# Longer lags in three attention stages of a four-layer transformer kernel

## The reference

```python
x = x + xattn0(norm(x), ctx, ctx, mask, bias)      # 16 heads, softmax, stage a0
x = x + rwkv_ffn(norm(x))                          # stage f0
x = x + gelu(norm(x) @ ctx.T) @ ctx                # stage m1
x = x + top2_experts(norm(x))                      # stages r1, e1
x = x + xattn2(norm(x), ctx, ctx, causal)          # 16 heads, stage a2
x = x + shared_ffn(norm(x)) + top1_expert(norm(x)) # stages r2, s2, e2
x = x + xattn3(norm(x), ctx, ctx)                  # scores that are 0 count as -1e30, stage a3
x = x + int8_linear(norm(x))                       # one scale for the whole tensor, stage q3

def xattn(x, ...):
    q, k, v = heads(x @ Wq), heads(ctx @ Wk), heads(ctx @ Wv)   # 16 heads of 16
    return softmax(q @ k.T / 4 + bias) @ v @ Wo
```

## Time and profile before

| | before |
|---|---|
| median of 3 runs | 1209.71 us (1206.89 to 1211.71) |
| the profiled execution | 1210.15 us, span 1208.4 us |
| mean granted TensorE clock | 0.853 of full speed |
| PE busy | 919.9 us, 76% |
| DVE busy | 578.3 us, 48% |
| ACT busy | 412.9 us, 34% |
| POOL busy | 403.8 us, 33% |

### The profile page before, as it was taken

The page is one execution under the profiler, slowest core; times in us unless marked ns, Lnnn a source line. Parts: engine busy times, 40 slices in busy tenths (PEclk is TensorE's granted clock), DMA queues, the critical chain, the costliest instruction groups (busy, mean ns, idle before and its releaser), DMA issues. The chain is left out here.

```text
span 1208.4 us, 18723 instructions
## 1 busy us (share of the span) xinstructions
PE 919.9 (76%) x5575; PEld 607.7 (50%) x5576; DVE 578.3 (48%) x1230; ACT 412.9 (34%) x804; POOL 403.8 (33%) x739
## 2 busy tenths in 40 slices
PE   7688758776249999945678749997999977787732
PEld 5465537642127777723455415564666664555511
DVE  4788835644322222227998532221111136768827
ACT  4345533322003233314666422221222216555610
POOL 5556635431560000036775211100000025555512
PEclk9799978968559999975988769998999968788955
DMA  5780000000121111127410030002111110000002
GB/s 166 263 295 2 1 22 26 0 9 0 66 91 52 63 63 61 61 68 261 175 32 10 1 107 30 22 18 66 44 46 50 40 28 15 14 15 6 1 1 69
DMA packets 60182, 71.25 MB, mean 59 GB/s; under 512 B 8171, under 2 KB 51923, under 8 KB 60115
## 3 DMA queue, kind: packets, MB, share of 16 engines
q1 hardware_dynamic: 55507, 57.81, 14.4%
q0 software_dynamic: 4608, 12.59, 3.2%
HBM read 45.73 MB, written 24.64 MB: 58 GB/s over the span
## 5 line engine op out<-in xcount | busy, mean ns | idle before, releaser
L1549 PE MATMUL PS<-WE,tmp 128*128 x496 | 185.8, 518 | 0.0
L1193 DVE TENSOR_TENSOR tmp<-PS,tmp 128x352 f32<-128x352 f32 (+1 forms) x78 | 47.4, 608 | 260.2 <-ACT tmp L851 260.2
L540 POOL TENSOR_TENSOR tmp<-tmp,small 128x616 f32<-128x616 f32 x96 | 116.5, 1214 | 107.3 <-DVE small L969 104.0
L505 POOL DMA_INDIRECT WE<-ys,slot_u x32 | 32.5, 1016 | 341.2 <-DMA ys<-tmp 335.3
L1549 PEld LDWEIGHTS PS<-WE,tmp 128*128 128x128 f32 x496 | 91.5, 194 | 60.4 <-issue 36.2
L764 ACT ACTIVATE tmp<-PS 128x768 f32<-128x768 f32 x96 | 77.8, 810 | 112.2 <-PE PS L1373 111.5
L851 ACT ACTIVATE tmp<-PS 128x352 f32<-128x352 f32 (+1 forms) x78 | 41.4, 530 | 218.7 <-PE PS L1549 218.7
L1569 PE MATMUL PS<-WE,tmp 128*128 (+1 forms) x418 | 101.0, 380 | 2.1 <-DVE tmp L1205 2.1
L1284 PE MATMUL PS<-ident,XN 128*128 128x128 f32 x240 | 49.5, 342 | 67.7 <-ACT XN L700 53.7
L1371 PE MATMUL PS<-ident,tmp 128*128 128x128 f32 x384 | 69.6, 311 | 40.1 <-POOL rsx L527 21.8
L635 POOL DMA_INDIRECT xs<-tmp,slot_u x48 | 46.5, 969 | 121.2 <-DVE tmp L1180 111.5
(11 more groups left out here) (204 smaller groups left out, 1623.6 us busy)
## 6 DMA issues: line engine op xcount, KB each, us to landing
tmp<-xs SPq DMA_DIRECT2D x62, 128.0 KB, 2.0
ys<-tmp SPq DMA_DIRECT2D x62, 128.0 KB, 1.7
xs<-WE SPq DMA_DIRECT2D x4, 1536.0 KB, 9.5
WE<-in_L_w SPq DMA_DIRECT2D x16, 352.0 KB, 7.1
WE<-in_L_rgT SPq DMA_DIRECT2D x8, 512.0 KB, 9.9
WE<-in_L_ruT SPq DMA_DIRECT2D x8, 512.0 KB, 10.0
WE<-in_L_rdT SPq DMA_DIRECT2D x8, 512.0 KB, 10.2
X<-in_x SPq DMA_DIRECT2D x8, 256.0 KB, 6.7
```

The source lines that it names most:

```text
L540: pool.tensor_tensor(sc, sc, spread(mx[:, q], SK), ALU.add).then_inc(shifted, 1)
L1193: dve.tensor_tensor(HH[:, q, 0:F], PS[:, 2 * q + 1, 0:F], SL[:, q, 0:F], ALU.mult).then_inc(hh_ready, 1)
L1549: last = pe.matmul(PS[:, 2 * q + k, 0:F], XS[:, q, c], w, start=c == 0, stop=c == G - 1)
```

## The change

The slot tables move. Transposes of a unit stand three slots after its scores instead of two, values five instead of three. The copy of the transposed values (ACT) goes to slot k+4. ACT empties `BANK_X` one slot after PE has filled it (`later(...)`), where it used to do so in the same slot; `out_projection` moves from 4b+7 to 4b+10 and so stands in the slot right behind `queries(b+3)`. Norms go one slot later than their statistics, and `XN` gets a second buffer. On POOL the shift of slot s goes ahead of the bias add and of the norm's arithmetic, and `MEANS` is written only for the output norms in `a2`. Gathers start one slot earlier, their add two slots earlier: in `a2` the last gather of batch entry b moves from slot 4b-8 to 4b-9, its add from 4b-6 to 4b-8. The value blocks of `a3` go from slot 0 to the slots -5 and -4 on PE and to -7 and -4 on DVE. No matmul or vector operation is added or taken away but 40 tiny copies to `MEANS`.

```diff
-        XN = sb("XN", [P, T, D])
+        XN = sb("XN", [P, 2, T, D])
...
         def queries_slot(b):
-            return UNITS * (b - 1) + 1
+            return UNITS * b - 3
         def out_proj_slot(b):
-            return UNITS * b + 7
+            return UNITS * b + 10
         def residual_slot(b):
-            return UNITS * b + 8
+            return UNITS * b + 11
         def deviations_slot(b):
-            return UNITS * b + 9
+            return UNITS * b + 12
+        def normalise_slot(b):
+            return UNITS * b + 13
         def transpose_slot(b):
-            return UNITS * b + 10
+            return UNITS * b + 15
         def gather_slot(b, t, k, K):
-            return UNITS * b - 11 + t * 2 + k * (2 // K)
+            return UNITS * b - 12 + t * 2 + k * (2 // K)
         def add_slot(b):
+            return UNITS * b - 8
+        def in_deviations_slot(b):
+            return UNITS * b - 7
+        def in_normalise_slot(b):
             return UNITS * b - 6
-        def in_deviations_slot(b):
-            return UNITS * b - 5
...
+        def later(slot_of):
+            return lambda b: slot_of(b) + 1
...
-                    bq = batch_at(queries_slot, s)
-                    if bq is not None and bq > 0 and stage != "a2":
-                        queries(bq)
...
-                    if 2 <= s < NU + 2:
-                        u = s - 2
+                    if 4 <= s < NU + 4:
+                        u = s - 4
                         act.wait_ge(pt_psum, u0 + u + 1)
                         after(act, ot_ready, (u0 + u) // 2 - 1 if u >= 4 else 0)
                         act.activation(PT[:, u % 4], PT_PSUM, ACT.Copy).then_inc(pt_ready, 1)
...
+                    bq = batch_at(later(queries_slot), s)
+                    if bq is not None and stage != "a2":
+                        queries(bq)
+                    for slot_of, which in ((later(in_transpose_slot), "in"), (later(transpose_slot), "out")):
...
-                    if s == 0 and stage == "a3":
-                        for i in range(B // 2):
-                            value_blocks(2, i)
+                    if stage == "a3" and s in (add_slot(0) + 1, add_slot(1)):
+                        for i in range(2):
+                            value_blocks(2, i if s < add_slot(1) else 2 + i)
...
-                    if 3 <= s < NU + 3:
-                        values(s - 3)
+                    if 5 <= s < NU + 5:
+                        values(s - 5)
...
-                    if 2 <= s < NU + 2:
-                        transposes(s - 2)
+                    if 3 <= s < NU + 3:
+                        transposes(s - 3)
```

More of the change, by code:

```diff
@@ L282, in slots_of @@
         def slots_of(stage):
-            return range(gather_slot(0, 0, 0, 1) if stage in FED_FROM else 0, transpose_slot(B - 1) + 1)
+            return range(gather_slot(0, 0, 0, 1) if stage in FED_FROM else queries_slot(0), later(transpose_slot)(B - 1) + 1)
         def norm_order(stage):
@@ L540, in attention @@
                         pool.tensor_tensor(sc, sc, spread(mx[:, q], SK), ALU.add).then_inc(shifted, 1)
+                    if j == 2 and 1 <= b <= B and stage != "a3":
+                        if stage in FED_FROM:
+                            pool.wait_ge(xn_ready, norms + order["in", b - 1] + 1)
+                        pool.tensor_tensor(x_of(b - 1), x_of(b - 1), repeat(rows[:, 1], T), ALU.add).then_inc(out_bias, 1)
+                    for slot_of, which in ((in_deviations_slot, "in"), (deviations_slot, "out")):
+                        bd = batch_at(slot_of, s)
+                        if bd is not None and (which, bd) in order:
+                            i = order[which, bd]
+                            deviations_and_shifts(norms + i, bd, shifts + i, stage == "a2" and which == "out")
                     if stage in FED_FROM:
@@ L764, in attention @@
                         act.activation(PT[:, u % 4], PT_PSUM, ACT.Copy).then_inc(pt_ready, 1)
[L765 to L768, removed]
-                        normalise(norms + i, bn, shifts + i, XN)
-                    bi = batch_at(in_deviations_slot, s)
-                    if bi is not None and stage in FED_FROM:
-                        i = order["in", bi]
-                        after(act, xt_psum, norms + i)
-                        if stage == "a3" and bi > 3:
-                            act.wait_ge(amax_taken, bi - 3)
-                        normalise(norms + i, bi, shifts + i, XN)
+                    bq = batch_at(later(queries_slot), s)
+                    if bq is not None and stage != "a2":
+                        queries(bq)
+                    for slot_of, which in ((later(in_transpose_slot), "in"), (later(transpose_slot), "out")):
+                        bt = batch_at(slot_of, s)
+                        if bt is not None and (which, bt) in order:
+                            xt_evacuate_at(norms + order[which, bt], bt)
+                    for slot_of, which in ((in_normalise_slot, "in"), (normalise_slot, "out")):
+                        bn = batch_at(slot_of, s)
+                        if bn is not None and (which, bn) in order:
+                            i = order[which, bn]
+                            after(act, xt_psum, norms + i - 1)
+                            if stage == "a3":
+                                after(act, amax_taken, sum(w == "out" for (w, _), n in order.items() if n <= i - 2))
+                            normalise(norms + i, bn, shifts + i, XN[:, i % 2])
                 end_stage(act, stage)
@@ L1403, in attention @@
                 for s in slots_of(stage):
-                    if s == 0 and stage == "a3":
-                        for i in range(B // 2):
+                    if stage == "a3" and s in (in_transpose_slot(0) - 1, in_transpose_slot(0)):
+                        for i in range(2) if s < in_transpose_slot(0) else range(2, 4):
                             pe.wait_ge(v_ready, B // 2 + i + 1)
                             value_blocks(2, i)
-                    if s == 0 and stage != "a2":
-                        queries(0)
                     if s == 0 and stage == "a3":
```

55 lines of the change are left out of this document (18 added, 37 removed).

## The result

| | before | after |
|---|---|---|
| median | 1208.36 us | 1259.97 us (1254.91 to 1267.59, 4 runs) |
| ratio after / before | | 1.0428, 95% interval 1.0362 to 1.0495 |
| the profiled execution | 1210.15 us | 1256.2 us, span 1254.5 us |
| mean granted TensorE clock | 0.853 | 0.830 |

What follows compares the result with a forecast made beforehand. It took `a0` as nearly TensorE's, `a2` as VectorE's and `a3` as a ring of waits. `a0` +6.8, `a2` +14.3, `a3` -13.4 and clock +12 gave +19.7 on 1210.15: 1229 us, range 1205 to 1244.

Steps and rivals of the forecast that it cites:

- The ring through the bank: Output projection waits for ScalarE to empty `BANK_X` behind exponential and copy: 15.6 us an entry in `a0`, 19.5 in `a3`.
- TensorE waits for the copy: Sign expected in the changed profile: TensorE's transposes wait for the ScalarE copy, 20 us and more in `a0`.
- the copy's own ring: Transposes wait for the copy behind the exponential, the next reciprocal sums for them: 3.16 us a slot, VectorE alone 2.56.
- The faster rival: Early copy removes TensorE's 0.43 us wait per unit if the exponential starts under about 1.4 us after B(s-1): 1188 us; 15%.
- The value blocks run at full clock: Start of `a3`: value blocks moved ahead of the rows take 6.9 us at full clock; first biased scores 11.2 us earlier.
- Unit 8 of `a2`: First stalls of `a2`, gathers under a weight load: unit 8 would come 6.7 us later.
- The step that failed in `a0`: Clock term of `a0`: taken as 0, with bounds of 0 and 4 us, as its gaps come apart.
- In `a3`, where the clock was booked at 9 us: Clock term of `a3`: a third of the time at half clock, 1.5 us by 6 entries, 9 us.
- Plain slots cost 0.5 and the projection 0.3 more: Entry of `a2`: these two costs beside the gather's stall; 16.65 us becomes 18.8.
- the stall is 1.4 us: Entry of `a2`: VectorE's add waits 1.4 us for the last gather, which has one slot to land instead of two.
- The ends: Ends of the three attentions: -1 us in `a0`, -1.5 in `a2`, -1 in `a3`.
- two without outputs: Entries of `a3` without outputs: 16.1 us each, where a full entry takes 19.5.

Runs made afterwards that it cites:

- filler: Changed kernel with four identity transposes added on TensorE beside the values in nearly every slot; 1234.56 us, 1.0213 of the kernel before.
- copy_mid: Changed kernel with ScalarE's copy, in `a2` alone, between the exponential and the two small copies; 1247.97 us, 1.0317 of the kernel before.
- both_undone: Changed kernel with `BANK_X` emptied in the slot of its fill, ahead of the copy, and the copy of unit s-3 in slot s; 1197.71 us.
- bank_same_slot: Changed kernel with ScalarE emptying `BANK_X` in the slot of its fill, still behind exponential and copy; 1219.02 us, 1.0101 of the kernel before.
- gap_filled: both_undone with 20 identity transposes in TensorE's long wait in five slots of `a2`; 1195.08 us, 0.986 of the kernel before.
- adds_one_later: both_undone with the adds of gathered rows, their statistics' rest and norm one slot later; 1182.39 us, 0.9772 of the kernel before.
- after_adds_later: Changed kernel with the adds of gathered rows, their statistics' rest and norm one slot later; 1254.17 us, 1.0367 of the kernel before.

## Why the forecast was wrong

**Right.** The ring through the bank, which runs through the copy in ScalarE's queue, is there with the size given: 15.8 us an entry in `a0` at full clock for 15.6, 19.15 and 19.36 in `a3` for 19.5. TensorE waits for the copy (19.5 us in `a0`, "20 us and more" was written). Whether the copy's own ring takes 3.16 us a slot no row shows by itself; at full clock it bound no full entry of `a0` (14.61 us with or without it). The faster rival failed by its own condition: the exponential starts 2.2 us after the end of the biased scores in the middle of `a0`, as before the change, where the rival needed 1.4. The value blocks run at full clock ahead of the rows, and bring 10.9 us for 11.2:

```profile
1017.68 1.03 PE L1328 MATMUL PS<-WE,firstrows 77*128 77x256 f32 x4
...
1024.92 1.03 PE L1328 MATMUL PS<-WE,leftrows 77*128 77x256 f32 x4
1025.78 0.60 PE L1285 MATMUL PS<-ident,XN 128*128 128x128 f32 x4
```

Unit 8 of `a2` is 6.3 us later for 6.7, in part by luck. By the forecast the fourth add would have begun 47.4 us behind the first gather, and unit 8 would have come 13.6 us behind it. The add began at 45.1 us, and the way from there to unit 8 took 15.5 us, at a clock of 0.50.

**The step that failed in `a0`: "In `a0` the clock was 1.00; bounds are 0 and 4 us (a third of 1.99 by 6), and I take 0, as its gaps come apart."** The clock of the kernel before was used for a kernel whose waits are longer. Four of the six windows from unit 8 on ran at 0.61 to 0.81. The term was 6.8 us by the run with filler, above even the upper bound, which had counted the projection alone: queries, transposes, scores and values double as well. In `a3`, where the clock was booked at 9 us, it measured 9.4.

The page TensorE: Matmul & The Clock Gate of the Trainium skill, on the second failure mode, had said what the rows of `a0` then showed: idle gaps between groups of matmuls make the clock swing. The forecast set it aside for the 1.00 of the earlier trace rows. Gaps alone don't decide, as the kernel before shows: with one of 0.43 us in every slot five entries in a row ran at 1.00.

**The step that failed in `a2`: "Plain slots cost 0.5 and the projection 0.3 more", and "the stall is 1.4 us".** Plain slots were priced by the ring of `a0`, with only the exponential ahead of the copy. ScalarE's small copies of `a2` stand ahead of it as well, and they wait for VectorE. That is 13.3 us by copy_mid, the fall of the clock behind this wait with it. The gather's stall, in exchange, is 0.2 us an entry behind unit 8 instead of 1.4: the longer entry gave the gather its time. Two errors of opposite sign left +6.1 where they met.

**The ends.** -1, -1.5 and -1 were credited for the tails; they came out at +0.7, +2.6 and +0.3. These three and the head of `a0` make some 7 us, and no row carried them. In `a3` the first two entries took 36.0 us where two without outputs were forecast at 16.1 each: 3.8 of the 5.0 us that are left there.

**What stays open.** Over both_undone the bank alone costs 1.6%, the copy alone 1.9%, the two together 5.2%. At full clock a part of the rest is there in `a0`, 0.35 us an entry; what is left of it should be the clock, but that is an inference, and no run held the clock and varied the rings. Why the fall of the clock follows one wait of TensorE and not another is open too: in both_undone it came behind waits of 1.65 and 0.67 us, in bank_same_slot a wait of 1.92 us left an entry of `a0` at 1.00.

## What to carry to other kernels

A lag in slots says nothing until the queue of each engine that it passes is read: find what now stands ahead of the instruction whose result another engine waits for, in every stage that shares the code, since one stage had two more instructions there. A stage which runs at full clock before a change will not stay there if the change makes TensorE's waits longer; book the lower clock on every matmul of the ring. And take a change of many parts apart: this one held a gain of 0.9% (longer lags, moved blocks), 2.3% with its adds a slot later, behind the places of two instructions on ScalarE.

## What the runs showed of the hardware

The same instructions at the same place got different clocks. both_undone, gap_filled and adds_one_later are the same program up to `a2`. The first was profiled on one chip, the other two on a second. The entry of `a0` from unit 16 on, first both_undone, then gap_filled:

```profile
100.97:115.24 14.27, 12.07 (x140) 8.56 (x140) 12.11 (x25) 8.08 (x15) 9.16 (x17) 1.00 0.01 2
```

```profile
102.56:119.69 17.13, 14.94 (x140) 10.34 (x140) 12.10 (x24) 8.19 (x15) 9.24 (x17) 0.80 0.01 2
```

That is 2.9 us in one entry, and 85.4 against 95.8 us over units 8 to 31 (89.2 in adds_one_later), with no instruction of `a0` changed: more than most single edits here did to `a0`, so that a stretch says little without its clock beside it. It isn't so in every kernel: the changed kernel, after_adds_later and copy_mid, which share their `a0`, took 98.3, 98.1 and 97.7 us. Part 1 of the page TensorE: Matmul & The Clock Gate of the Trainium skill tells that the moment at which the clock changes differs from run to run. The rows of both_undone and gap_filled agree. And over 300 matmuls of no use made the changed kernel 2% faster.
